# A recommender tower on one core: the first chunk's shifted rows and eight of its pair tiles made by TensorE instead of copied by DMA

## The chip, the cores and the metric

One core of one Trainium2 chip runs the program. The metric is the device time of one execution in microseconds, median over the runs. The core has TensorE (matmuls), VectorE, ScalarE and GpSimd, and SP, which only issues DMAs; ScalarE and GpSimd issue DMAs too. In the profile they are PE (PEld for its weight loads), DVE, ACT, POOL and SP.

## The reference

Each of 2048 rows of `ids` picks one row of 16 numbers from each of 39 tables. Three interaction layers follow, in which every pair of a field of the input and a row of the last layer's output is multiplied and summed with a weight:

```python
e = jnp.stack([tbl_0[ids[:, 0]], ..., tbl_38[ids[:, 38]]], axis=1)      # (2048, 39, 16)
x0 = xk = e
for idx, (W, b) in enumerate(params):                                   # W: (39, K, 128), K = 39, 64, 64
    z = jnp.einsum('bhd,bkd,hks->bsd', x0, xk, W) + b[None, :, None]
    z = jax.nn.relu(z)
    if idx != n_layers - 1:
        xk = z[:, :64, :]
        direct.append(z[:, 64:, :])
    else:
        direct.append(z)
logit = jnp.sum(jnp.concatenate(direct, axis=1), axis=-1)               # (2048, 256)
h = jnp.concatenate([logit, dense_ctx], axis=1)
h = jnp.maximum(h @ W_top1 + b_top1, 0.0)
h = jnp.maximum(h @ W_top2 + b_top2, 0.0)
y = h @ W_top3
```

All arrays are float32.

## The kernel before

The batch is cut into 16 groups of 128 rows, and each group into 4 chunks of 32 rows, so that a chunk has 32 times 16 = 512 columns. For a group, GpSimd gathers the 39 fields' rows into `emb` (128 partitions, one row of the batch each), one indirect DMA per field. SP stores `emb` into `x0_transposed` in HBM, in which a field is a row and batch times 16 are the columns. It has 39 rows and the first 20 of them once more, so that a block that is shifted by up to 20 fields can be read straight.

From there a chunk is loaded twice. `x0_diag` has 7 tiles for layer 0: three bands of 39 partitions, each holding the fields shifted by 0 to 20 (`diag_band`: SP loads two bands, ScalarE the third), and an eighth tile with the unshifted rows. `x0_pairs` has 20 tiles for layers 1 and 2: tile t holds field 2t in the upper 64 partitions and field 2t + 1 in the lower 64 (`pairs_half`: SP loads one half, ScalarE the other; SP also loads tile 19, which holds field 38 in all). There are two such buffers, for even and odd chunks.

VectorE multiplies four tiles at a time by `xk` (`product`), into a ring of four slots `prod`. TensorE multiplies them by weights and sums in `z`, in PSUM. Some tiles go as plain f32 (two passes each), others are split into a high part, rounded by ScalarE (`hi_parts`), and a low part, subtracted by VectorE or GpSimd (`lo_parts`), with three single passes. In layer 2 nearly all low parts are GpSimd's. The slots take their tiles in the order 0, 4, 16, 8, 12 (`FIRST_TILE`). TensorE's order in a chunk is layer 1 of this chunk, layer 0 of the next, layer 2 of this one. ScalarE turns a finished `z` into the next `xk` (`hand_on`), and every engine runs its own list in order and waits on semaphores.

GpSimd's gathers for the next group are set by numbers: `GATHERS_AHEAD` = 20 of group 1 come before its loop, and `GATHERS_AT` puts 10, 9, 10 and 10 into the four chunks of a group, each batch between its low part of layer 1 and its low parts of layer 2; the last two are for the group after.

Ahead of the loop the first chunk runs alone: SP stores group 0, waits for the store, loads the bands of chunk 0, waits for them and loads the pair tiles. VectorE and TensorE do layer 0 of chunk 0 in the meantime. The products of layer 1 wait for all pair tiles (`x0_pairs_in`) and for `xk1`.

## Time and profile before

| | us |
|---|---|
| median of 3 runs | 2450.69 (2449.82 to 2453.27) |
| profiled execution, its own time | 2460.42 |
| its span, first to last instruction | 2458.7 |
| TensorE busy | 2359.5 |
| VectorE busy | 2250.7 |
| GpSimd busy | 1710.2 |
| ScalarE busy | 1497.6 |

A span is the time from the first to the last instruction of the profiled execution, and the times of single instructions are counted from its start. Busy times leave out waits and the issuing of DMAs by SP and ScalarE. Matmuls overlap, so that the durations of single ones can add up to more than the time they take together; the chain counts each moment once.

### The profile page before, as it was taken

To read this page: it belongs to the slowest core of one execution; us is meant where nothing else is said; L and a number is where in the kernel's file an instruction comes from. 1 tells how busy PE (TensorE), PEld (TensorE's weight loads), DVE (VectorE), ACT (ScalarE), POOL (GpSimd) and SP (SyncE) were. 2 spreads that over 40 slices of the span, in tenths; PEclk is the share of its full clock that TensorE was granted. 3 is DMA by queue.
4 is the path that set the end of the run, shared out by engine and by line. 5 is a ranking of instruction groups with operands and counts; after the bars stand their busy time and mean duration, and the time that the engine had idled before them with its cause. 6 is when DMAs were issued, how large, how long until landed. Compare 5 with 4: busy or idle time off the path is not lost.

```text
span 2458.7 us, 26866 instructions
## 1 busy us (share of the span) xinstructions
PE 2359.5 (96%) x7768; PEld 1463.9 (60%) x7768; DVE 2250.7 (92%) x1383; ACT 1497.6 (61%) x1791; POOL 1710.2 (70%) x1091
## 2 busy tenths in 40 slices
PE   0499999999999999999999999999999999999999
PEld 0266666666666666666666666666666666666656
DVE  0499999999999999999999999999999999999983
ACT  0366666666666666666666666666666666666655
POOL 6577777777877777777777777677777767754540
PEclk9899999999999999999999999999999999999999
DMA  2887887878778787878878787887878788787730
GB/s 70 238 208 190 223 219 180 222 205 207 188 220 221 175 228 205 203 193 223 218 180 223 205 208 188 221 215 177 229 207 197 197 217 216 181 227 205 194 104 1
DMA packets 381242, 481.11 MB, mean 196 GB/s; under 512 B 140715, under 2 KB 155803, under 8 KB 381141
## 3 DMA queue, kind: packets, MB, share of 16 engines
q1 hardware_dynamic: 260294, 275.13, 44.4%
q10 hardware_dynamic: 100480, 200.29, 29.6%
q0 software_dynamic: 20448, 5.45, 1.9%
q8 instruction: 9, 0.15, 0.0%
q14 instruction: 11, 0.09, 0.0%
HBM read 470.96 MB, written 9.84 MB: 196 GB/s over the span
## 4 chain that ended last, share of the span: by engine, by line
PE 87%; POOL 4%; issue 4%; DMA 1%; DVE 1%; ACT 1%; SPq 0%; POOLq 0%; ACTq 0%; DVEq 0%
PE z L846 43%; PE z L825 42%; POOL lo_parts L273 4%; DVE prod L516 1%; PE z L963 1%; DMA x_pairs<-x_transposed 1%; PE xk L963 1%; ACT hi_parts L657 1%; POOL half_parts L267 0%; PE direct L963 0%; ACT xk L678 0%; DMA x_transposed<-emb 0%; ACT xk L677 0%; POOLq L139 0%; SPq L321 0%
## 5 line engine op out<-in xcount | busy, mean ns | idle before, releaser
L516 DVE TENSOR_TENSOR prod<-x_pairs,xk 128x2048 f32<-128x2048 f32 x640 | 1438.6, 2281 | 87.3 <-PE z L846 36.5
L825 PE MATMUL z<-prod,w_plain 128*128 128x512 f32 (+2 forms) x2688 | 1263.8, 594 | 93.5 <-DVE prod L516 93.4
L273 POOL TENSOR_TENSOR lo_parts<-prod,hi_parts 128x1024 fp32r<-128x1024 f32 x384 | 918.1, 2391 | 487.7 <-ACT hi_parts L657 462.4
L657 ACT CAST hi_parts<-prod 128x1024 fp32r<-128x1024 f32 x766 | 797.1, 1048 | 698.8 <-DVE prod L516 493.8
L846 PE MATMUL z<-hi_parts,w_lo 128*128 128x512 f32 (+1 forms) x1536 | 866.6, 564 | 3.2 <-POOL lo_parts L273 2.0
L446 POOL DMA_INDIRECT emb<-in_tbl,idx x624 | 702.5, 1126 | 195.5 <-issue 180.3
L825 PEld LDWEIGHTS z<-prod,w_plain 128*128 128x128 f32 (+2 forms) x2688 | 510.6, 190 | 492.5 <-issue 411.7
L846 PE MATMUL z<-hi_parts,w_hi 128*128 128x512 f32 (+1 forms) x1536 | 610.1, 397 | 0.0
L846 PE MATMUL z<-lo_parts,w_hi 128*128 128x512 f32 (+1 forms) x1536 | 606.8, 395 | 0.0
L846 PEld LDWEIGHTS z<-hi_parts,w_lo 128*128 128x128 f32 (+1 forms) x1536 | 289.9, 189 | 208.4 <-issue 146.1
L846 PEld LDWEIGHTS z<-lo_parts,w_hi 128*128 128x128 f32 (+1 forms) x1536 | 291.0, 189 | 191.4 <-issue 152.5
L846 PEld LDWEIGHTS z<-hi_parts,w_hi 128*128 128x128 f32 (+1 forms) x1536 | 288.8, 188 | 68.8
L273 DVE TENSOR_TENSOR lo_parts<-prod,hi_copy 128x1024 fp32r<-128x1024 f32 x256 | 310.2, 1212 | 12.7 <-ACT hi_copy L671 12.2
L516 DVE TENSOR_TENSOR prod<-x_diag,xk 117x2048 f32<-117x2048 f32 (+1 forms) x128 | 256.7, 2006 | 58.1 <-issue 58.1
L671 ACT CAST hi_copy<-prod 128x1024 fp32r<-128x1024 f32 x256 | 259.4, 1013 | 2.0 <-DVE lo_parts L273 0.3
L677 ACT ACTIVATE xk<-z,columns 64x512 f32<-64x512 f32 x128 | 83.0, 648 | 155.6 <-PE z L846 137.4
L273 DVE TENSOR_TENSOR lo_parts<-prod,hi_parts 117x1024 fp32r<-117x1024 f32 x128 | 150.1, 1210 | 0.0
L267 POOL TENSOR_TENSOR half_parts<-prod,half_parts 64x512 fp32r<-64x512 f32 x64 | 81.6, 1275 | 5.5
L678 ACT ACTIVATE xk<-z,columns 64x512 f32<-64x512 f32 x128 | 83.5, 652 | 1.6
L653 ACT CAST half_parts<-prod 128x512 fp32r<-128x512 f32 x128 | 78.5, 614 | 0.0
L701 ACT COPY xk<-x_diag 117x512 f32<-117x512 f32 x64 | 37.3, 583 | 59.4 <-DMA x_diag<-x_transposed 59.4
L846 PE MATMUL z<-half_parts,w_hi 128*128 128x512 f32 x128 | 50.8, 397 | 0.0
(75 smaller groups left out, 579.2 us busy)
## 6 DMA issues: line engine op xcount, KB each, us to landing
x_pairs<-x_transposed SPq DMA_DIRECT2D x64, 2432.0 KB
x_pairs<-x_transposed ACTq DMA_DIRECT2D x64, 2432.0 KB
x_diag<-x_transposed SPq DMA_DIRECT2D x128, 546.0 KB
x_diag<-x_transposed ACTq DMA_DIRECT2D x64, 546.0 KB
x_pairs<-x_transposed SPq DMA_DIRECT2D x64, 256.0 KB
emb<-in_tbl,idx POOLq DMA_INDIRECT x624
x_diag<-x_transposed SPq DMA_DIRECT2D x128, 78.0 KB
x_transposed<-emb SPq DMA_DIRECT2D x16, 312.0 KB, 6.1
```

What stands on the lines that cost most here:

```text
L267: engine.tensor_tensor(half_parts[0:HALF], held[0:HALF, at, :], hi, ALU.subtract).then_inc(done, 1)
L273: engine.tensor_tensor(lo_parts[0:rows, place:place + m, :], held[0:rows, at:at + m, :], hi, ALU.subtract).then_inc(done, 1)
L446: nc.gpsimd.indirect_dma_start(out=emb[:, f * D:(f + 1) * D], out_offset=None, in_=tables[f], in_offset=bass.IndirectOffsetOnAxis(ap=idx[: ...
L516: nc.vector.tensor_tensor(prod[0:rows, pos % RING, 0:n, :], a, xk.unsqueeze(1).broadcast_to([rows, n, N]), ALU.mult).then_inc(prod_ready, 1)
L653: nc.scalar.copy(half_parts[:], held[:, at, :]).then_inc(hi_ready, 1)
L657: nc.scalar.copy(hi_parts[0:rows, place:place + m, :], held[:, at:at + m, :]).then_inc(hi_ready, 1)
L671: nc.scalar.copy(hi_copy[:, 0:m, :].bitcast(F32R), held[:, at:at + m, :]).then_inc(hi_copied, 1)
L677: nc.scalar.activation(xk[0:HALF], z[layer][0:HALF], ACT.Relu, bias=b[0:HALF])
L678: nc.scalar.activation(xk[HALF:P], z[layer][0:HALF], ACT.Relu, bias=b[0:HALF]).then_inc(xk_ready[layer], 1)
L825: return nc.tensor.matmul(z[n][:], w, held[0:rows, i, :], start=first, stop=last)
L846: ins = nc.tensor.matmul(z[n][:], w, x, start=(first and i == 0), stop=(last and i == len(terms) - 1))
L963: ins = nc.tensor.matmul(acc[0:w.shape[1]], w, x, start=(k == 0 and not begun), stop=(k == len(terms) - 1))
```

## The change

In chunk 0 the seven shifted tiles of `x0_diag`, the unshifted rows for `xk0`, and tiles 12 to 19 of `x0_pairs` no longer come by DMA. TensorE transposes the first 32 rows of `emb` (16 small transposes into `z[1]`), VectorE copies the result to `rows0` (39x512), and TensorE multiplies `rows0` by matrices of zeros and ones, which pick for every output partition its field. Each result goes to one of three PSUM banks in turn, and ScalarE copies it to its tile. The matrices `by_diag` and `by_pair` are copied by VectorE out of `ident`, a twofold identity that GpSimd makes before its first gather. Tiles 0 to 11 are still copied by DMA, both halves from ScalarE's queue.

SP stores the first 32 rows of group 0 apart (`first_stored`), and the other 96 behind them; ScalarE's copies of tiles 0 to 11 wait for the first only. For later chunks nothing changes in how rows are stored and loaded.

Of group 1's gathers 14 instead of 20 come before the loop, 12 in chunk 0 and 13 in chunk 1. For that GpSimd's and VectorE's group 0 are written out ahead of their loops.

```diff
-GATHERS_AHEAD = 20
+GATHERS_AHEAD = 14
+GATHERS_FIRST = [range(14, 26), range(26, F), range(0, 10), range(10, 20)]
 GATHERS_AT = [range(20, 30), range(30, F), range(0, 10), range(10, 20)]
+SPREAD_PAIRS = (16, 17, 18, 19, 12, 13, 14, 15)
+COPIED_PAIRS = 12
+SPREAD_EARLY = 3
...
+        spread_banks = [z[1], hi_copy[:, 0, :], hi_copy[:, 1, :]]
+        spread_to = ([x0_diag[0:R0, t, :] for t in range(T0)]
+                     + [x0_pairs[0][:, t, :] for t in SPREAD_PAIRS])
...
+            def first_chunk():
+
+                sp.wait_ge(gathered, 16 * F)
+                store_rows(sp, 0, 0, slice(0, CB), first_stored)
+                store_rows(sp, 0, 0, slice(CB, P), xt_stored)
+                sp.wait_ge(xt_stored, 16 * ST_DMAS)
...
-            store_group(0)
-            sp.wait_ge(w0_summed, 2)
-            sp.wait_ge(w_split, 3)
-            load_chunk(0, 0)
+            first_chunk()
...
         def _(pool):
+            nc.gpsimd.memset(ident[:], 0.0).then_inc(ident_zero, 1)
+            for i in range(2):
+                pool.wait_ge(ident_zero, i + 1)
+                nc.gpsimd.affine_select(out=ident[:], in_=ident[:], compare_op=ALU.not_equal,
+                                        fill=1.0, base=i * F, pattern=[[-1, F + WRAP]],
+                                        channel_multiplier=1
+                                        ).then_inc((ident_zero, ident_ready)[i], 1)
...
             load_indices(1)
+            pool.wait_ge(first_stored, 16 * ST_DMAS)
+            pool.wait_ge(rows0_turned, 1)
             start_group(1, False)
             gather(range(0, GATHERS_AHEAD))
-            with pool.Fori(0, GROUPS - 2) as bt:
+            group(0, GATHERS_FIRST)
+            with pool.Fori(1, GROUPS - 2) as bt:
                 group(bt, GATHERS_AT)
...
+            dve.wait_ge(rows0_turned, 1)
+            nc.vector.tensor_copy(rows0[:], z[1][0:F]).then_inc(rows0_ready, 1)
             dve.wait_ge(xk0_ready, 1)
-            late, split = products(0, x0_diag, xk0, 0, 0, [], 0, 0)
+            late, split = products(0, x0_diag, xk0, 0, 0, [], 0, 0, {0: QUAD, 1: T0})
             subtract(late, split)
...
+            def take_spread(items):
+                for i in items:
+                    rows = spread_to[i].shape[0]
+                    act.wait_ge(spread, i + 1)
+                    nc.scalar.copy(spread_to[i], spread_banks[i % len(spread_banks)][0:rows]
+                                   ).then_inc(spread_ready, 1)
+
             act.wait_ge(weights_in, 16 * WEIGHT_DMAS)
-            act.wait_ge(xt_stored, 16 * ST_DMAS)
-            act.wait_ge(w0_summed, 2)
-            act.wait_ge(w_split, 3)
-            diag_band(nc.scalar, chunk_columns(0, 0), DIAG - 1)
-            copy_xk0(0)
-            pairs_half(nc.scalar, chunk_columns(0, 0), 0, 1)
+            act.wait_ge(gathered, 16 * F)
+            take_spread(range(0, 1))
+            act.wait_ge(first_stored, 16 * ST_DMAS)
+            for half in range(2):
+                src = xt[half:half + 2 * COPIED_PAIRS, 0:N].rearrange(
+                    "(t two) n -> t two n", two=2)[:, 0, :]
+                nc.scalar.dma_start(x0_pairs[0][half * HALF:(half + 1) * HALF, 0:COPIED_PAIRS, :],
+                                    src.partition_broadcast(HALF)).then_inc(first_pairs_in, 16)
+            take_spread(range(1, T0))
             for (k, at, m, _), place in zip(SPLITS[0], PLACES[0]):
...
+            take_spread(range(T0, T0 + SPREAD_EARLY))
             hand_on(0, xk1, b0_sb, SL0)
             direct_0()
+            take_spread(range(T0 + SPREAD_EARLY, len(spread_to)))
+            act.wait_ge(spread_ready, len(spread_to))
+            act.wait_ge(xt_stored, 16 * ST_DMAS)
             load_last_band(0, 1)
...
+            def spread_rows(items):
+                for i in items:
+                    if i >= len(spread_banks):
+                        pe.wait_ge(spread_ready, i + 1 - len(spread_banks))
+                    rows = spread_to[i].shape[0]
+                    nc.tensor.matmul(spread_banks[i % len(spread_banks)][0:rows], spread_by[i],
+                                     rows0[:], start=True, stop=True).then_inc(spread, 1)
+
+            pe.wait_ge(ident_ready, 1)
+            pe.wait_ge(gathered, 16 * F)
+            for d in range(D):
+
+                ins = nc.tensor.transpose(z[1][0:F, d:N:D], emb[0:CB, d:F * D:D], ident[0:CB, 0:CB])
+            ins.then_inc(rows0_turned, 1)
+            pe.wait_ge(chosen_ready, T0 + 3)
+            pe.wait_ge(rows0_ready, 1)
+            spread_rows(range(QUAD))
+            nc.tensor.matmul(xk0[0:R0], by_diag[:, T0, :], rows0[:], start=True, stop=True
+                             ).then_inc(xk0_ready, 1)
+            spread_rows(range(QUAD, T0 + SPREAD_EARLY))
             pe.wait_ge(w0_summed, 2)
             pe.wait_ge(w_split, 3)
             pe.wait_ge(weights_in, 16 * WEIGHT_DMAS)
             layer0(0, 0, {V: 0, G: 0})
+            spread_rows(range(T0 + SPREAD_EARLY, len(spread_to)))
+            pe.wait_ge(spread_ready, len(spread_to))
```

TensorE's list began with layer 0 of chunk 0 (the three rows of `w0_plain`). Now this stands ahead of it, from its first matmul on:

```order
L981 MATMUL z1<-ident,emb 39x32 x16
L974 MATMUL z1<-rows0,by_diag 117x512
L974 MATMUL hi_copy<-rows0,by_diag 117x512 x2
L974 MATMUL z1<-rows0,by_diag 117x512
L986 MATMUL xk2<-rows0,by_diag 117x512
L974 MATMUL hi_copy<-rows0,by_diag 117x512 x2
L974 MATMUL z1<-rows0,by_diag 117x512
L974 MATMUL hi_copy<-rows0,by_pair 128x512 x2
L974 MATMUL z1<-rows0,by_pair 128x512
L903 MATMUL z0<-prod,w0_plain 128x512 x3
```

Sixteen transposes and eleven matmuls of 512 columns now stand ahead of layer 0; five more stand behind it, ahead of layer 1.

ScalarE's list from the end of its weight casts to its first high part of the loop, before:

```order
L281 DMA x_diag<-x_transposed 39x7x512
L282 DMA x_diag<-x_transposed 39x512
L701 COPY xk<-x_diag 117x512
L287 DMA x_pairs<-x_transposed 64x19x512
L729 CAST hi_parts<-prod 117x1024 x2
L677 ACTIVATE xk<-z,columns 64x512
L678 ACTIVATE xk<-z,columns 64x512
L704 ACTIVATE direct<-z,columns 64x512
L281 DMA x_diag<-x_transposed 39x7x512
L282 DMA x_diag<-x_transposed 39x512
```

And now, from the first copy behind the casts of layer 0 on (lines 788 are copies of spread tiles, 741 and 742 the hand-on of `xk1`, 319 and 320 the band of chunk 1):

```order
L803 CAST hi_parts<-prod 117x1024 x2
L788 COPY x_pairs<-hi_copy 128x512 x2
L788 COPY x_pairs<-z 128x512
L741 ACTIVATE xk<-z,columns 64x512
L742 ACTIVATE xk<-z,columns 64x512
L768 ACTIVATE direct<-z,columns 64x512
L788 COPY x_pairs<-hi_copy 128x512 x2
L788 COPY x_pairs<-z 128x512
L788 COPY x_pairs<-hi_copy 128x512 x2
L319 DMA x_diag<-x_transposed 39x7x512
L320 DMA x_diag<-x_transposed 39x512
```

Five copies now stand between `direct_0` and the band of chunk 1, and three ahead of the hand-on.

GpSimd's list from its first gather to the low parts of layer 2 of chunk 0, before:

```order
L446 DMA emb<-in_tbl,idx 128x16 x39
L434 DMA idx<-in_ids 128x39
L446 DMA emb<-in_tbl,idx 128x16 x20
...
L273 TENSOR_TENSOR lo_parts<-prod,hi_parts 128x1024
L446 DMA emb<-in_tbl,idx 128x16 x10
```

And now, to those of chunk 1:

```order
L463 MEMSET ident 39x59
...
L466 AFFINE_SELECT ident<-ident 39x59 x2
L485 DMA emb<-in_tbl,idx 128x16 x39
L473 DMA idx<-in_ids 128x39
L485 DMA emb<-in_tbl,idx 128x16 x14
L290 TENSOR_TENSOR lo_parts<-prod,hi_parts 128x1024
L485 DMA emb<-in_tbl,idx 128x16 x12
L290 TENSOR_TENSOR lo_parts<-prod,hi_parts 128x1024 x3
L284 TENSOR_TENSOR half_parts<-prod,half_parts 64x512
L290 TENSOR_TENSOR lo_parts<-prod,hi_parts 128x1024 x3
L485 DMA emb<-in_tbl,idx 128x16 x13
```

Three instructions stand ahead of the first gather, and six of group 1's gathers moved from ahead of the first low part to behind it, two into chunk 0 and four into chunk 1.

## Rows read from the trace of the kernel before

**Rows 1.** The page, part 1: busy time, share of the span, instructions.

```profile
PE 2359.5 (96%) x7768; PEld 1463.9 (60%) x7768; DVE 2250.7 (92%) x1383; ACT 1497.6 (61%) x1791; POOL 1710.2 (70%) x1091
```

**Rows 2.** Timeline of GpSimd, 0 to 135 us: start, us, what [idle before].

```profile
3.00 1.08 POOL L446 DMA_INDIRECT emb<-in_tbl,idx  x1 [2.42 <-DMA idx<-in_ids]
...
52.34 0.94 POOL L446 DMA_INDIRECT emb<-in_tbl,idx  x1 [0.30 <-issue]
...
62.56 0.99 POOL L446 DMA_INDIRECT emb<-in_tbl,idx  x1 [7.04 <-DMA x_transposed<-emb]
...
108.61 2.36 POOL L273 TENSOR_TENSOR lo_parts<-prod,hi_parts 128x1024 fp32r<-128x1024 f32 x1 [20.35 <-ACT hi_parts L657]
...
111.13 0.96 POOL L446 DMA_INDIRECT emb<-in_tbl,idx  x1 [0.15 <-issue]
...
119.90 2.82 POOL L446 DMA_INDIRECT emb<-in_tbl,idx  x1 [0.31 <-issue]
...
126.08 7.36 POOL L273 TENSOR_TENSOR lo_parts<-prod,hi_parts 128x1024 fp32r<-128x1024 f32 x3 [0.85 <-ACT hi_parts L657]
```

**Rows 3.** Timeline of SP's queue, 0 to 135 us.

```profile
54.68 0.40 SPq L336 DMA_DIRECT2D x_transposed<-emb  x1
...
72.97 0.73 SPq L287 DMA_DIRECT2D x_pairs<-x_transposed  x1
```

**Rows 4.** Timeline of ScalarE and its DMA queue, 0 to 135 us.

```profile
72.98 0.59 ACT L701 COPY xk<-x_diag 117x512 f32<-117x512 f32 x1 [59.44 <-DMA x_diag<-x_transposed]
...
85.67 0.65 ACT L677 ACTIVATE xk<-z,columns 64x512 f32<-64x512 f32 x1 [7.76 <-PE z L846]
...
101.08 0.64 ACTq L287 DMA_DIRECT2D x_pairs<-x_transposed  x1
...
101.84 1.04 ACT L657 CAST hi_parts<-prod 128x1024 fp32r<-128x1024 f32 x1 [14.18 <-DVE prod L516]
```

**Rows 5.** Timeline of VectorE, 0 to 135 us.

```profile
73.60 3.95 DVE L516 TENSOR_TENSOR prod<-x_diag,xk 117x2048 f32<-117x2048 f32 x2 [58.06 <-issue]
...
98.59 4.49 DVE L516 TENSOR_TENSOR prod<-x_pairs,xk 128x2048 f32<-128x2048 f32 x2 [18.18 <-DMA x_pairs<-x_transposed]
```

**Rows 6.** Timeline of TensorE, its layer 0 parts in five places.

```profile
77.70 5.13 PE L825 MATMUL z<-prod,w_plain 117*128 117x512 f32 x6 [77.70 <-DVE prod L516]
...
120.89 2.74 PE L825 MATMUL z<-prod,w_plain 117*128 117x512 f32 x6
...
156.66 1.88 PE L825 MATMUL z<-prod,w_plain 117*128 117x512 f32 x4
...
1626.99 1.45 PE L825 MATMUL z<-prod,w_plain 117*128 117x512 f32 x3
...
1663.27 2.74 PE L825 MATMUL z<-prod,w_plain 117*128 117x512 f32 x6
```

**Rows 7.** The chain that ended last, 0 to 200 us: start, us, what.

```profile
121.06 2.58 PE z L825 x6
...
123.63 2.80 PE z L846 x12
```

**Rows 8.** Timeline of GpSimd, in chunk 1 and near 1633 us.

```profile
161.84 7.38 POOL L273 TENSOR_TENSOR lo_parts<-prod,hi_parts 128x1024 fp32r<-128x1024 f32 x3 [2.39 <-ACT hi_parts L657]
...
1632.84 7.37 POOL L273 TENSOR_TENSOR lo_parts<-prod,hi_parts 128x1024 fp32r<-128x1024 f32 x3 [1.65 <-ACT hi_parts L657]
```

**Rows 9.** Windows: length; busy us of PE, PEld, DVE, ACT, POOL; clock, DMA share, GB/s.

```profile
76.00:80.00 4.00, 2.30 (x3) 1.17 (x4) 3.89 (x4) 1.91 (x2) 3.08 (x4) 1.00 0.97 235
92.00:96.00 4.00, 0.00 (x0) 0.00 (x0) 0.00 (x0) 0.00 (x0) 0.00 (x0) 0.50 1.01 235
96.00:98.50 2.50, 0.00 (x0) 0.00 (x0) 0.00 (x0) 0.00 (x0) 0.00 (x0) 0.50 0.88 196
101.00:109.60 8.60, 8.09 (x12) 3.92 (x13) 7.72 (x5) 6.10 (x7) 0.99 (x1) 0.50 0.99 229
104.00:121.80 17.80, 17.29 (x50) 10.43 (x50) 17.80 (x12) 11.78 (x15) 10.90 (x9) 0.84 1.01 289
```

More of the change, by code:

```diff
@@ L274, in low_part, with chosen, store_rows @@
                                      hi, ALU.subtract).then_inc(done, 1)
+        spread_banks = [z[1], hi_copy[:, 0, :], hi_copy[:, 1, :]]
+        spread_to = ([x0_diag[0:R0, t, :] for t in range(T0)]
+                     + [x0_pairs[0][:, t, :] for t in SPREAD_PAIRS])
+        def chosen(first, *dims):
+            rows = ident[0:F, first:]
+            return bass.AP(tensor=rows.tensor, offset=rows.offset, ap=[rows.ap[0], *dims])
+        pair_columns = by_pair[:].rearrange("f g h -> f (g h)")
+        spread_by = ([by_diag[:, t, :] for t in range(T0)]
+                     + [pair_columns[:, (t - COPIED_PAIRS) * P:(t + 1 - COPIED_PAIRS) * P]
+                        for t in SPREAD_PAIRS])
+        def store_rows(engine, bt, first, parts, done):
+            cols = xt[:, bass.ds(first, P * D)].rearrange("f (b d) -> b f d", d=D)
+            rows = emb[:].rearrange("p (f d) -> p f d", d=D)
+            engine.dma_start(cols[parts, 0:F, :], rows[parts]).then_inc(done, 16)
+            engine.dma_start(cols[parts, F:F + WRAP, :], rows[parts, 0:WRAP, :]).then_inc(done, 16)
         def diag_band(engine, chunk, i):
@@ L349, in load_chunk @@
                     sp.wait_ge(xt_stored, 16 * ST_DMAS * (bt + 1))
-                if not (isinstance(bt, int) and bt == c == 0):
-                    sp.wait_ge(summed2, sums)
+                sp.wait_ge(summed2, sums)
                 chunk = xt[:, bass.ds(first, N)]
@@ L357, in load_chunk @@
                     store_group(bt + 1)
[L358 to L364 removed]
+                sp.wait_ge(prod_ready, slots)
                 pairs_half(sp, chunk, c, 0)
@@ L540, in splits_of, with products @@
                 return here
-            def products(n, copies, xk, slot, pos, late, split, chunk):
+            def products(n, copies, xk, slot, pos, late, split, chunk, spread_in={}):
                 first_tile, rows, tiles = (FIRST_TILE, P, TX) if n else (L0_FIRST, R0, T0)
                 for k, first in enumerate(first_tile):
+                    if k in spread_in:
+                        dve.wait_ge(spread_ready, spread_in[k])
                     product(slot + k, pos + k, copies[0:rows, first:min(first + QUAD, tiles), :],
@@ L582, in group @@
                     copies = x0_pairs[c % 2]
-                    dve.wait_ge(x0_pairs_in[c % 2],
-                                16 * X0_PAIRS_DMAS * (bt * (CHUNKS // 2) + c // 2 + 1))
+                    first = isinstance(bt, int) and bt == c == 0
+                    if first:
+                        dve.wait_ge(first_pairs_in, 32)
+                        dve.sem_inc(x0_pairs_in[0], 16 * X0_PAIRS_DMAS)
+                    else:
+                        dve.wait_ge(x0_pairs_in[c % 2],
+                                    16 * X0_PAIRS_DMAS * (bt * (CHUNKS // 2) + c // 2 + 1))
                     dve.wait_ge(xk_ready[0], chunk + 1)
-                    late, split = products(1, copies, xk1, slot, pos, [], split, chunk)
+                    spread_in = {FIRST_TILE.index(t): T0 + QUAD * (i + 1)
+                                 for i, t in enumerate(SPREAD_PAIRS[::QUAD])} if first else {}
+                    late, split = products(1, copies, xk1, slot, pos, [], split, chunk, spread_in)
                     slot, pos = slot + SLX, pos + SLX
@@ L604, in group @@
                     subtract(late, split)
-            with dve.Fori(0, GROUPS - 1) as bt:
+            group(0, False)
+            with dve.Fori(1, GROUPS - 1) as bt:
                 group(bt, False)
```

34 lines of the change are left out of this document (25 added, 9 removed).

## The prediction

> **What bounds the kernel now.** I read the page first. TensorE is busy 96% of the span [rows 1], so the middle of the run can only become shorter if TensorE gets less to do, and the change touches nothing there. The timelines of the first 135 us come next, with the wait ahead of each row in brackets at its end: TensorE waits 77.7 us for its first matmul [rows 6], and VectorE 18.2 us for the pair tiles of chunk 0 [rows 5]. Up to there it is a chain in which TensorE hardly works. GpSimd issues the 39 gathers one per 1.25 us from 3.00 to 53.3 [rows 2]; SP stores the rows at 54.68 and copies the pair tiles from 72.97, when the diagonal copies have landed [rows 3]; ScalarE copies `xk0` at 72.98 and hands `xk1` on with two activations from 85.67 to 87.0 [rows 4]; VectorE starts layer 0 at 73.60, but its first layer 1 product (call that moment T1) only at 98.59 [rows 5]. So `xk1` lay ready for 11.6 us: two things, the pair tiles and the layer 0 chain, must both come earlier.
>
> Behind T1 TensorE takes over. Its layer 0 part of the loop's chunks starts (call it s) at 120.89 and 156.66 [rows 6], 35.77 us apart. The chain gives the warm prices: 2.58 us for six f32 passes (0.43 each, two passes to a matmul) and 2.80 us for twelve of the others [rows 7]: 42 f32 passes and 76 others make 35.8 us, so no time is lost there. What the start saves is therefore kept to the end, unless GpSimd, whose low parts TensorE needs in layer 2, makes it wait. That margin is small and can be read. Let p be the start of GpSimd's first layer 2 low part. At s = 120.89, p is 126.08 [rows 2], p - s = 5.19, and the next s comes 35.77 later: no stall. At s = 1626.99, p is 1632.84 [rows 8], p - s = 5.85, and the next s is 36.28 later [rows 6]: 0.51 lost. So each us of p beyond s + 5.35 costs TensorE one us, and the next s is p + 30.4.
>
> **The change, part by part.**
>
> Removed: the diagonal copies of chunk 0 (54.7 to 73.0, behind the store), and 8 of 20 pair tiles. Left are 12 tiles by 128 partitions by 2 KB, 3.1 MB. While such copies ran alone the queues moved 235 GB/s [rows 9]: 13.4 us. They start when the first 32 rows are stored. Before, both stores had landed by 62.5 [rows 2], 7.9 us after the issue, for 128 rows; a quarter of the rows cannot take longer, nor less than the 0.9 us of two issues. I take 58.5 (about half of the 7.9), so the tiles are in at about 58.5 + 0.7 for the issue + 13.4 = 72.6, and at 76.6 if the store takes its full 7.9 us.
>
> Added ahead of T1, from 54.7 on:
> - Sixteen transposes. No row shows so small a matmul. Above, each is two passes of the 0.233 us kind (2.80 / 12), 7.5 us in all; below, they go by columns (32 of 512), 0.03 us each, 0.5 us in all. I take one such pass each, 0.2 us, nearer the upper row since each also loads its own weights: 3.2 us.
> - One VectorE copy of 39x512. The nearest row is ScalarE's copy of 117x512 at 0.59 us [rows 4]; with two handovers 0.9 us. So the spreads start at 58.8.
> - Ahead of layer 0, eleven f32 matmuls (seven shifted tiles, `xk0`, three pair tiles). Warm each is 0.86 us, 9.5 us. Cold they cost twice as much: the first six passes of the run before took 5.13 us [rows 6] against 2.58 warm [rows 7]. The granted clock stands at 1.00 there [rows 9], but a pass of 0.855 us is that of the 1.2 GHz level, and TensorE had done nothing until then. From there until TensorE's rate doubled it ran 4.5 us (77.70 to about 82.2); after the pause before T1 the column stands at 0.50, the 1.2 GHz level, and stays so to about 109.6 while TensorE works from 100.94 on [rows 9]. A slow spell of 4.5 us costs 2.25 us of work, one of 8.7 us costs 4.3. I take 2.5: 12.0 us, until 70.8. ScalarE's copies (0.6 us, three banks) are faster than the matmuls and hide beside them. VectorE's two layer 0 products (3.95 us together [rows 5]) wait for the fifth and eighth matmul and end at about 70.5, so they are hidden as well.
> - Layer 0 itself, warm: 2.58 + 2.80 = 5.4 us, until 76.2; the hand-on 1.4 us (85.6 to 87.0 before). T1 = 77.6. With the low ends (0.5 us, all warm) it is 72.4, when the tiles decide at 72.6; with the high ends (7.5 us, 4.3 us cold) 83.7.
>
> The Trainium skill (TensorE: Matmul & The Clock Gate, Part 4) says that transposes in transpose mode do not count as work for the clock gate. By that rule the matmuls behind them start cold, as in the trace's own first passes, and the sum stays as it stands; were the transposes to count, 3.2 us of the spell would pass under them, and T1 would be about 1.6 us earlier.
>
> Added behind T1. ScalarE still owes five copies when layer 0 ends. In order: hand-on to +1.3 us, `direct_0` to +2.0, three copies to +3.8, two more to +5.1 (TensorE makes them between +2.7 and +4.4). Its sequencer then waits for all 15 copies before it issues the diagonal pair of DMAs (about 0.9 us) and the pairs half (0.64 us [rows 4]), so the first high part begins at about +6.9, that is T1 + 5.5, where before it was 101.84 - 98.59 = 3.25 behind T1. VectorE's first low part waits for it: 2.25 us. From there VectorE works without a gap to 122 in the run before [rows 9], so the third product, and GpSimd's first low part with it, slips as much: from T1 + 10.0 [rows 2] to T1 + 12.3.
>
> Moved: six gathers of group 1 from ahead of the loop into chunks 0 and 1. GpSimd is ahead of time before T1, so there the six save nothing; in the chunks they lie right ahead of the low parts of layer 2. Chunk 0 had 10: from 111.13 to 125.23, 14.1 us (ten steps of 1.25 and one long gather of 2.82 us [rows 2]), and 0.85 us to spare. Twelve take 16.6. So p = T1 + 12.3 + 2.4 + 0.15 + 16.6 + 0.1 = T1 + 31.5, and the next s = T1 + 61.9. Before it was 156.66 - 98.59 = T1 + 58.1. Loss 3.8 us, the 2.25 above included. It also covers TensorE, which would otherwise start its first loop part 1 to 2 us late. Chunk 1 had 9 gathers and 2.39 us to spare [rows 8]; 13 take four more, 5.0 us, so p slips by 2.6 us, from s + 5.18 to s + 7.8, and 2.45 us are lost; with the L1 low part a little later, 2.6. From chunk 2 on the batches are those of before.
>
> The ten copies that VectorE gets ahead of the transposes and the three instructions of GpSimd ahead of the gathers I cost at nothing: VectorE idles for 58.1 us before 73.6 [rows 5], and GpSimd waits 2.42 us for the indices [rows 2]. Without that cover GpSimd's three would cost their own length, one for one. SP's and ScalarE's loads of chunk 1 are released by the same instructions as before and keep their distance to T1, so they stay hidden.
>
> **Sum.** T1: 77.6 - 98.6 = -21.0. Chunk 0: +3.8. Chunk 1: +2.6. Net -14.6 us. The profiled execution spans 2458.7 us and is timed at 2460.4, the median of the runs is 2450.7; the 10 us between lie over the whole run, so I subtract from the median: 2436.1. The changed profile's span should be about 2444.
>
> **The rivals.**
> 1. The copied pair tiles decide T1. For it: 64-byte stores of the other 96 rows and GpSimd's gathers run beside them, and the copies start no earlier than the first store lands. Against: 5 us of margin at my values. If the store takes its 7.9 us and the rate falls to the 196 GB/s of the last stretch before T1 [rows 9] (15.8 us), they land at 62.6 + 0.7 + 15.8 = 79.1: T1 +1.5; with 4 us of crowding by the store +5. Time 2438 to 2441. Chance 0.12.
> 2. TensorE's part is slow: transposes at their upper price and all eleven matmuls at 1.2 GHz, T1 = 54.7 + 7.5 + 0.9 + 18.8 + 5.4 + 1.4 = 88.7. Time up to 2447, likelier 2442. Chance 0.08.
> 3. GpSimd's new selects must first load code, and the gathers start late, one for one, beyond 2.42 us. Against: GpSimd's first elementwise instruction at 108.61 took 2.36 us, no more than a third of the three later ones' 7.37 [rows 2, 8], so nothing was loaded there. If a load came to twice the 2.42 us it would cost 2.4: 2438.5. Chance 0.06. The Trainium skill (GPSIMD Engine Reference, 2.1 Instruction dispatch) gives about 6 us for the first call to a freshly loaded kernel; by it the time would be about 2440.
> 4. Slower than before: ScalarE stands before `first_stored` with one tile copied, and TensorE has three banks; it stops after three matmuls until ScalarE goes on. Each us that the first store lands beyond about 62 then costs one. The whole gain is spent if it lands at 76, 22 us after its issue; 128 rows took at most 7.9. Time above 2451. Chance 0.02.
> 5. The mechanism holds but GpSimd, late twice, does not catch up with the index load of group 2, and further chunks lose as well. A loss like chunk 1's in each of the next four gives 10 us back: 2446. Against: the index load comes 22 us behind s and moves with it. Chance 0.04.
>
> **How the numbers follow.** The forecast, 2436.1, has 0.68, with T1 between 72.6 and 82: 2431 to 2441. The range for 8 in 10 adds most of rivals 1 and 3 above: 2430 to 2443. A difference under 0.2% (4.9 us) cannot be told from none. Faster by more takes the forecast and rivals 1 and 3, and most of 2: 0.93. Within it rival 5 and the rest of 2: 0.05. Slower: 0.02.
>
> **What the changed profile would show.** Transposes from 54.7, rows copy near 58, spreads to 71; the first layer 1 product at 77.6 and not released by a DMA; ScalarE's first high part 5.5 us behind it; p - s of about 7 and 8 in chunks 0 and 1, then 5.2; the waits of TensorE for GpSimd's low parts up by some 4 to 6 us in all. T1 beyond 84 would prove the chain wrong, p - s near 5.2 in chunk 1 the gathers' price.

## The result and the profile after

| | us |
|---|---|
| median of 4 runs, kernel before | 2450.94 (2449.82 to 2453.27) |
| median of 4 runs, changed kernel | 2440.08 (2439.63 to 2440.62) |
| ratio | 0.9958, interval 0.9946 to 0.9971 |
| profiled execution, its own time | 2440.03 |
| its span | 2438.3 |

The change saves 10.9 us of the predicted 14.6; the time lies inside the range of 2430 to 2443. The mechanism is the predicted one. One term of the sum, TensorE's slow spell, was far too small; the transposes were cheaper than taken, and some 5 us of the saving stand in no trace. So the number came into the range partly by luck.

The page's first part, against [rows 1]: TensorE is 13.5 us longer busy: 24.6 us more up to the first layer 0 part of the loop (52.0 against 27.4), and 11.1 us less behind it.

```profile
PE 2373.0 (97%) x7816; PEld 1466.3 (60%) x7816; DVE 2254.5 (92%) x1394; ACT 1505.0 (62%) x1805; POOL 1718.0 (70%) x1094
```

The timeline of TensorE to the first layer 1 product, against [rows 6] (start, us, what; the wait ahead in brackets). A row of x2 is one f32 matmul in two passes, a row of x4 two matmuls.

```profile
54.76 1.27 PE L981 MATMUL z<-ident,emb 32*39 32x32 f32 x16 [54.76 <-DMA emb<-in_tbl,idx]
56.89 2.02 PE L974 MATMUL z<-rows,by_diag 39*117 39x512 f32 x2 [0.87 <-DVE rows L626]
58.72 3.61 PE L974 MATMUL hi_copy<-rows,by_diag 39*117 39x512 f32 x4
...
70.66 3.61 PE L974 MATMUL hi_copy<-rows,by_pair 39*128 39x512 f32 x4
74.08 1.91 PE L974 MATMUL z<-rows,by_pair 39*128 39x512 f32 x2
75.92 5.13 PE L903 MATMUL z<-prod,w_plain 117*128 117x512 f32 x6
80.41 0.86 PE L924 MATMUL z<-hi_parts,w_lo 117*128 117x512 f32 x1
81.11 0.40 PE L924 MATMUL z<-lo_parts,w_hi 117*128 117x512 f32 x1
81.35 0.39 PE L924 MATMUL z<-hi_parts,w_hi 117*128 117x512 f32 x1
```

Read the starts, not the durations, since matmuls overlap. From 56.89 to 75.92 there are 22 passes in 19.0 us, 0.86 us each, the price of the 1.2 GHz level. The six passes of layer 0 cost the same (5.13, as in [rows 6]). Only from 80.4 on are the steps 0.23 us. TensorE had been at work for 23.5 us by then, without a pause after 56.9.

The same stretch in windows: length, busy us of each engine, and the granted clock behind POOL.

```profile
64.00:72.00 8.00, 8.00 (x11) 3.02 (x10) 2.77 (x2) 2.86 (x5) 2.32 (x3) 1.00 1.10 204
72.00:80.00 8.00, 8.00 (x10) 2.83 (x9) 4.03 (x4) 3.04 (x5) 6.17 (x7) 1.00 0.97 183
80.00:84.00 4.00, 4.00 (x15) 2.66 (x14) 0.00 (x0) 0.18 (x1) 3.07 (x4) 1.00 0.90 162
84.00:88.00 4.00, 4.00 (x9) 1.56 (x9) 2.84 (x2) 3.61 (x7) 1.89 (x2) 0.92 0.35 65
88.00:94.00 6.00, 5.03 (x6) 1.17 (x4) 1.65 (x1) 2.74 (x4) 0.00 (x0) 0.50 0.79 164
94.00:98.00 4.00, 2.62 (x10) 1.72 (x10) 3.75 (x3) 2.43 (x4) 0.00 (x0) 0.97 1.07 202
```

Between 64 and 80 the column says 1.00 and is not to be believed: some 19 passes in 16 us, with TensorE busy throughout, are the 1.2 GHz level (from 80 to 84 there are fifteen in 4 us). I take it that the column knows only changes; the first, by the passes, comes at 80.4, after 4.5 us of layer 0's 117 rows. From there on the column agrees with the passes. Note the fall between 84 and 94: layer 0 is over at 83.7, and TensorE goes on without a pause with the five late spreads, rows of 39.

VectorE, against [rows 5].

```profile
56.06 0.68 DVE L626 COPY rows<-z 39x512 f32<-39x512 f32 x1 [37.86 <-PE z L981]
65.78 2.29 DVE L558 TENSOR_TENSOR prod<-x_diag,xk 117x2048 f32<-117x2048 f32 x1 [9.04 <-PE xk L986]
71.52 1.75 DVE L558 TENSOR_TENSOR prod<-x_diag,xk 117x1536 f32<-117x1536 f32 x1 [3.45 <-ACT x_diag L788]
...
85.16 4.49 DVE L558 TENSOR_TENSOR prod<-x_pairs,xk 128x2048 f32<-128x2048 f32 x2 [9.03 <-ACT xk L742]
94.25 1.22 DVE L290 TENSOR_TENSOR lo_parts<-prod,hi_copy 128x1024 fp32r<-128x1024 f32 x1 [4.60 <-ACT hi_copy L735]
```

T1 is 85.16 instead of 98.59, and what it waits for is `xk1` of ScalarE, not a DMA. The first low part then waits 4.60 us for ScalarE, whose timeline follows, against [rows 4].

```profile
59.04 0.59 ACT L788 COPY x_diag<-z 117x512 f32<-117x512 f32 x1 [45.57 <-PE z L974]
59.06 1.43 ACTq L798 DMA_DIRECT2D x_pairs<-x_transposed  x2
...
83.82 0.65 ACT L741 ACTIVATE xk<-z,columns 64x512 f32<-64x512 f32 x1 [7.21 <-PE z L924]
...
89.43 0.59 ACT L788 COPY x_pairs<-hi_copy 128x512 f32<-128x512 f32 x1 [1.12 <-PE hi_copy L974]
90.04 0.60 ACTq L319 DMA_DIRECT2D x_diag<-x_transposed  x1
...
92.13 1.04 ACT L721 CAST hi_parts<-prod 128x1024 fp32r<-128x1024 f32 x1 [2.12 <-issue]
```

GpSimd, against [rows 2, 8]: selects, first gather of group 0, first gather of group 1, and the low parts of layer 2 in chunks 0 and 1.

```profile
1.26 0.60 POOL L466 TENSOR_SCALAR_AFFINE_SELECT ident<-ident 39x59 f32<-39x59 f32 x2 [0.24 <-POOL ident L463]
2.98 1.09 POOL L485 DMA_INDIRECT emb<-in_tbl,idx  x1 [1.12 <-DMA idx<-in_ids]
69.07 0.99 POOL L485 DMA_INDIRECT emb<-in_tbl,idx  x1 [13.59 <-DMA x_transposed<-emb]
...
117.23 7.51 POOL L290 TENSOR_TENSOR lo_parts<-prod,hi_parts 128x1024 fp32r<-128x1024 f32 x3
...
154.97 7.50 POOL L290 TENSOR_TENSOR lo_parts<-prod,hi_parts 128x1024 fp32r<-128x1024 f32 x3
```

And TensorE's layer 0 parts, from which s is read; the third follows at 185.69.

```profile
110.31 2.85 PE L903 MATMUL z<-prod,w_plain 117*128 117x512 f32 x6
147.98 2.74 PE L903 MATMUL z<-prod,w_plain 117*128 117x512 f32 x6
```

By these rows p is 6.92 and 6.99 behind s in the first two chunks, and the next s comes 37.67 and 37.71 later. Chunk 2 still takes 36.25; from the fifth chunk on most steps are 35.62.

### The profile page after: what moved, and what is told of

The parts are those of the page before. It is cut to its first block, busy times and chain, and to the rows that moved or that the text cites. A ratio compares the mean times of both kernels' runs of the same rounds, so it can differ in the third digit from the quotient of the medians.

```text
span 2438.3 us, 26914 instructions
## 1 busy us (share of the span) xinstructions
PE 2373.0 (97%) x7816; PEld 1466.3 (60%) x7816; DVE 2254.5 (92%) x1394; ACT 1505.0 (62%) x1805; POOL 1718.0 (70%) x1094
## 4 chain that ended last, share of the span: by engine, by line
PE 92%; POOL 4%; DVE 1%; issue 1%; DMA 1%; ACT 1%; POOLq 0%; ACTq 0%; DVEq 0%
PE z L903 45%; PE z L924 44%; POOL emb L485 2%; POOL lo_parts L290 2%; DVE prod L558 1%; PE z L1063 1%; PE xk L1063 1%; PE hi_copy L974 1%; DMA x_diag<-x_transposed 1%; PE direct L1063 0%; PE z L974 0%; ACT hi_parts L721 0%; DVE lo_parts L290 0%; POOL half_parts L284 0%; POOLq L143 0%
## 5 line engine op out<-in xcount | busy, mean ns | idle before, releaser
L290 POOL TENSOR_TENSOR lo_parts<-prod,hi_parts 128x1024 fp32r<-128x1024 f32 x384 | 927.6, 2416 | 456.2 <-ACT hi_parts L721 432.0
L924 PE MATMUL z<-lo_parts,w_hi 128*128 128x512 f32 (+1 forms) x1536 | 600.7, 391 | 0.0
L290 DVE TENSOR_TENSOR lo_parts<-prod,hi_copy 128x1024 fp32r<-128x1024 f32 x256 | 310.3, 1212 | 11.8 <-ACT hi_copy L735 5.9
L924 PE MATMUL z<-half_parts,w_lo 128*128 128x512 f32 x128 | 50.7, 396 | 0.0
```

What stands on the lines that cost most here:

```text
L290: engine.tensor_tensor(lo_parts[0:rows, place:place + m, :], held[0:rows, at:at + m, :], hi, ALU.subtract).then_inc(done, 1)
L924: ins = nc.tensor.matmul(z[n][:], w, x, start=(first and i == 0), stop=(last and i == len(terms) - 1))
```

## The experiments

The theory, called A below: TensorE's clock does not rise, and cannot be held, by matmuls whose operands have 39 rows, however close together they stand. The rival B: the clock would have risen, but started from idle, and matmuls ahead of the spreads would carry it over. Three groups of kernels ran, each group on one chip beside the kernel before. Where it matters the text says which.

### Spread operands of 128 rows

```diff
-        rows0 = sb("rows0", [F, N])
-        by_diag = sb("by_diag", [F, T0 + 1, R0])
+        rows0 = sb("rows0", [P, N])
+        by_diag = sb("by_diag", [P, T0 + 1, R0])
...
+            nc.vector.memset(rows0[:], 1.0).then_inc(wide_set, 1)
+            nc.vector.memset(by_diag[:].rearrange("p t r -> p (t r)"), 0.0).then_inc(wide_set, 1)
```

`by_pair` is treated alike. The 89 rows added are ones (in `rows0`) by zeros (in the matrices), so the sums stay the same. There are as many matmuls, with as many columns.

> The operands of the spread matmuls get all 128 rows instead of 39: below row 39 the moving operand holds ones and the matrices zeros, so the results are the same; VectorE's three fills lie in its idle time near 18 us. Theory A (the 39-row matmuls leave TensorE at 1.2 GHz, since it is the work in the array that raises its clock): the spreads start at 56.9, the passes take 0.85 us for 4.5 to 9 us and 0.43 after that, the eleven matmuls end at 68 to 71 instead of 75.9, layer 0 at 74 to 77, and the first layer 1 product starts at 78 to 79, held there by the pair tiles (their copies ran from 60.7 to 77.3). Time 6 us under the changed kernel, 2434. Rival B (the rows do not matter; two-pass matmuls in a row, or the pauses between them, keep the clock down): passes of 0.85 us up to layer 0 as before, first layer 1 product at 85.2, time 2440.

Measured: 2429.61 us, ratio 0.9917 (0.9903 to 0.9930) beside a kernel before at 2450.2. TensorE in this kernel:

```profile
53.61 1.27 PE L986 MATMUL z<-ident,emb 32*39 32x32 f32 x16 [53.61 <-DMA emb<-in_tbl,idx]
55.74 2.02 PE L979 MATMUL z<-rows,by_diag 128*117 128x512 f32 x2 [0.87 <-DVE rows L631]
57.57 3.11 PE L979 MATMUL hi_copy<-rows,by_diag 128*117 128x512 f32 x4
60.52 1.02 PE L979 MATMUL z<-rows,by_diag 128*117 128x512 f32 x2
...
67.53 2.81 PE L908 MATMUL z<-prod,w_plain 117*128 117x512 f32 x6
```

From 60.5 a matmul costs 0.86 us instead of 1.71, and layer 0 is at full rate from its first pass. The eleven spreads take 11.8 us (55.74 to 67.53), where I had 12.0, and 19.0 with 39 rows. The five late ones stay at full rate too (four passes in 1.98 us from 75.77, against 2.92 from 86.47 with 39 rows). A is confirmed for rows filled in this way. Whether it is their number or what they hold, no run tells: zeros in both operands were not tried. The time is 4.4 us under the 2434 expected; T1 came as expected, and 4.1 us were won between it and s (21.1 us instead of the changed kernel's 25.2). The next bound shows at once:

```profile
78.16 4.48 DVE L559 TENSOR_TENSOR prod<-x_pairs,xk 128x2048 f32<-128x2048 f32 x2 [7.86 <-DMA x_pairs<-x_transposed]
83.54 1.22 DVE L291 TENSOR_TENSOR lo_parts<-prod,hi_copy 128x1024 fp32r<-128x1024 f32 x1 [0.89 <-ACT hi_copy L740]
```

`xk1` was ready at 74.4; T1 waits for the copied pair tiles, my rival 1. ScalarE's late copies now fall into that wait, and its first high part is back at T1 + 3.26 (81.42).

> The kernel with spread operands of 128 rows once more, on one chip with the changed kernel. If the 39-row operands are what kept TensorE at its lower rate, it is 10 us (9 to 12) faster than after_again, at a ratio of 0.9917. If the gain of the first run came from something else of that chip, the two are equal.

> The changed kernel itself, as the base for the three others on the same chip. Expected 0.9958 of the kernel before, within 0.002; the first layer-1 product at 85 us, after the wait for xk1.

Measured, on one chip: 2430.55 us for it and, for the changed kernel run again, 2440.01. The ratios are 0.9921 (0.9908 to 0.9935) and 0.9962 (0.9948 to 0.9975), the kernel before 2449.74. So 9.5 us hang on the rows of the operands, though the matmuls are the same in number, columns and result. T1 was 78.83 and 84.96.

### Work ahead of the spreads

42 matmuls of 128x128x512 whose result nobody reads, started by GpSimd's 32nd gather:

```diff
+            pe.wait_ge(w_split, 3)
+            pe.wait_ge(nearly, 1)
+            for _ in range(42):
+                nc.tensor.matmul(z[1][:], w_hi[1][:, 0, :],
+                                 w_hi[1][:].rearrange("p t s -> p (t s)")[:, 0:N],
+                                 start=True, stop=True)
```

> TensorE multiplies 42 times 128x128 by 128x512 (results thrown away) in the last 11 us of the gathers; the spreads keep their 39 rows. Theory A: the clock is at its upper level when the transposes start at 54.8, and falls 3 to 4 us after the last full matmul although TensorE goes on with 39-row matmuls, as it fell 3.6 us after layer 0 in the changed kernel; so one to four passes are at 0.43 us and the rest at 0.85. First layer 1 product at 83 to 85, time 2438 to 2440. Rival B: the clock stays up as long as TensorE is busy at all, all spreads at 0.43 us, first layer 1 product at 78 (the pair tiles), time 2434.

> Both edits together. Theory A: all passes of the spreads at 0.43 us, eleven matmuls from 56.9 to 66.3, layer 0 ends at 72, xk1 is ready at 73.5, and VectorE now waits for the pair tiles until 78 to 79: the transfers and no longer TensorE set the first layer 1 product. Time like the wide kernel's or 1 us less, 2433. Rival C (the pair tiles are not what comes next, they were in much before 77): first layer 1 product at 73.6, time 2429.

Measured: 2438.73 (ratio 0.9952, 0.9939 to 0.9966) and 2429.62 (0.9918, 0.9904 to 0.9931). These tell nothing of B, by a fault in their design. The signal behind GpSimd's 32nd gather reached TensorE at 29.8, some 12 us before that gather's own row, so the matmuls came too early and left TensorE idle for 12.4 us:

```profile
29.82 12.68 PE L984 MATMUL z<-w_hi 128*128 128x512 f32 x42 [29.82 <-POOLq L524]
54.93 1.30 PE L990 MATMUL z<-ident,emb 32*39 32x32 f32 x16 [12.44 <-DMA emb<-in_tbl,idx]
```

With 98 of them there is no pause:

> As the warm kernel, which ended its full matmuls 12 us too early to tell anything, but with 98 of them, so that they last until about 54 us. Spreads at 39 rows. Theory A (39-row matmuls do not hold TensorE's clock up): it is at its upper level at the first spreads near 56.9 and falls 3 to 7 us after the last full matmul, near 58 to 61, so the first one to four passes take 0.43 us and the rest 0.85; first layer 1 product at 82 to 84.5, time 2437 to 2439. Rival B (any busy TensorE holds it): all passes 0.43 us, first layer 1 product at 78, time 2430 as the wide kernel.

Measured, on another chip, where the kernel before took 2466.34: 2470.41, ratio 1.0023 (1.0009 to 1.0036). The extra matmuls overran and held up the transposes by 6.5 us, so the time itself says little. The trace settles the question:

```profile
55.60 5.63 PE L984 MATMUL z<-w_hi 128*128 128x512 f32 x15 [0.84 <-issue]
61.16 1.28 PE L990 MATMUL z<-ident,emb 32*39 32x32 f32 x16
63.30 1.08 PE L977 MATMUL z<-rows,by_diag 39*117 39x512 f32 x2 [0.87 <-DVE rows L629]
64.22 1.88 PE L977 MATMUL hi_copy<-rows,by_diag 39*117 39x512 f32 x4
65.94 1.57 PE L977 MATMUL z<-rows,by_diag 39*117 39x512 f32 x2
67.31 1.91 PE L995 MATMUL xk<-rows,by_diag 39*117 39x512 f32 x2
...
79.39 4.79 PE L906 MATMUL z<-prod,w_plain 117*128 117x512 f32 x6
```

And its windows at 62 and 67, in the columns of above:

```profile
62.00:66.00 4.00, 3.13 (x14) 1.54 (x13) 0.68 (x1) 0.59 (x2) 1.92 (x2) 1.00 0.08 18
67.00:71.00 4.00, 4.00 (x6) 1.55 (x5) 1.75 (x1) 0.69 (x3) 3.00 (x4) 0.50 1.09 220
```

The spreads start at the 2.4 GHz level (0.43 a pass), and in the midst of them, with 39-row matmuls back to back, the granted clock falls to 0.50 and the passes go to 0.86. They stay there until layer 0. Ahead of the spreads stand the transposes and a pause of 0.87 us; the fall behind layer 0 in the changed kernel, above, has neither. So matmuls of 39 rows neither raise the clock nor hold it. B has fallen: warming saves 3 us, since the eleven spreads take 16.1 instead of 19.0 (63.30 to 79.39).

### Which pair tiles are copied

Two kernels: in `diag_only` all 20 tiles are copied and TensorE makes only the diagonal. `wide_copied16` is the wide kernel with 16 copied, and its edit is:

```diff
-SPREAD_PAIRS = (16, 17, 18, 19, 12, 13, 14, 15)
-COPIED_PAIRS = 12
+SPREAD_PAIRS = (16, 17, 18, 19)
+COPIED_PAIRS = 16
```

> One part of the change alone: TensorE makes the shifted rows, but all 20 pair tiles of chunk 0 are copied by DMA (three DMAs on ScalarE's queue behind the first store). Its queue moved 3.1 MB in 16.7 us in the changed kernel, 190 GB/s; 5.2 MB take 27.6 us from 60.7, so the first layer 1 product starts near 89 to 90 instead of 85.2, released by a DMA. ScalarE has no late copies, so its first high part lies 3.3 us behind that product, not 7.0, and 3.7 us of the 4 to 5 come back: time 2440 to 2441, the same as the changed kernel's. Rival: the eight tiles are what the change lives on, and without them the start is 8 us later: 2448.

> The wide kernel with tiles 0 to 15 copied and only 16 to 19 spread. If the copied tiles set its first layer 1 product (78.2, copies from 59.7 to 76.4), a third more bytes put it 5.5 us later, 83.7, and the time to 2434 to 2435, less up to 2 us because GpSimd's gathers of chunk 0 are then less late. Rival: the product waited for something else near 78 (the late copies of ScalarE); with four fewer of them it comes at 75 to 78: 2427 to 2430.

Measured, on the chip of 2466.34: 2463.70 (ratio 0.9993, 0.9984 to 1.0003) and 2459.10 (0.9974, 0.9964 to 0.9983). VectorE's first layer 1 product of the one and of the other:

```profile
89.18 4.48 DVE L558 TENSOR_TENSOR prod<-x_pairs,xk 128x2048 f32<-128x2048 f32 x2 [8.29 <-DMA x_pairs<-x_transposed]
```

```profile
87.42 4.49 DVE L559 TENSOR_TENSOR prod<-x_pairs,xk 128x2048 f32<-128x2048 f32 x2 [13.31 <-DMA x_pairs<-x_transposed]
```

Both wait for the copies, and T1 moves with their number: 12 tiles 78.2 (wide), 16 tiles 87.4, 20 tiles 89.2; behind the issue of the copies that is 20.3, 26.5 and 30.7 us. The issue of the 16 tiles came at 60.94, 3 us later than in wide, because VectorE copied the transposed rows only 3.2 us after the transposes; the profile puts that wait down to no engine of the core. T1 of `diag_only` is the one expected; that of `wide_copied16` was expected at 83.7. Both gained less in the time than expected (ratios of 0.996 and 0.9935).

With the diagonal alone T1 is 9.4 us before that of [rows 5] and the time the same as before. What the pair tiles are worth can't be read from the times, since the changed kernel was not run on this chip, and chunks there lose time in every kernel (below). The traces say more. Counted from SP's first store, the s of chunk 4 stands at 209.6 in the kernel before, 203.1 in the changed one and 204.4 in `diag_only` (264.24, 257.73 and 258.47 less 54.68, 54.64 and 54.06). So up to there the diagonal alone gives 5.2 of the 6.5 us, and the eight pair tiles, with 39 rows and late copies, 1.3. A surprise stood in `diag_only`, on ScalarE's queue:

```profile
58.49 1.80 ACTq L793 DMA_DIRECT2D x_pairs<-x_transposed  x2
60.33 9.14 ACTq L796 DMA_DIRECT2D x_pairs<-x_transposed  x1
69.51 1.07 ACT L784 COPY x_diag<-hi_copy 117x512 f32<-117x512 f32 x2 [10.46 <-issue]
```

The third DMA, tile 19, held ScalarE's sequencer for 9.14 us, so that the next copy came at 69.51 and the spreads, with three banks, stood still.

### When group 1 is gathered

The narrow kernel with the gathers of before, 20 ahead, then 10 and 9:

```diff
-GATHERS_AHEAD = 14
-GATHERS_FIRST = [range(14, 26), range(26, F), range(0, 10), range(10, 20)]
+GATHERS_AHEAD = 20
+GATHERS_FIRST = [range(20, 30), range(30, F), range(0, 10), range(10, 20)]
```

> Only the numbers of the gathers go back: 20 ahead of the loop, then 10, 9, 10, 10; the rest as changed. If the late low parts of GpSimd cost what the rule of the prediction says, p - s falls from 6.9 and 7.0 in chunks 0 and 1 to 5.2, and the 1.9 + 1.9 + 0.5 us that TensorE loses in chunks 0 to 2 come back: 2436. The 20 gathers run from 69.1 to 95.5 and end 3 us ahead of GpSimd's first low part at 98.9. Rival: they end late (another long gather) and hold that low part back, so that nothing is won: 2440.

Measured: 2435.45 (2434.94 to 2436.54), ratio 0.9941 (0.9928 to 0.9955), 4.6 us under the changed kernel's median; no run of the one reaches those of the other. They ran on two chips, on which the kernel before took much the same. By the traces 1.9 us of it is a T1 of 83.30, which the edit doesn't touch: the gathers ended 1.1 us earlier (transposes at 53.69), and TensorE's rate rose 0.8 us sooner in layer 0. Then 3.7 us fewer are lost in the first four chunks, and 1.4 us are given back between T1 and s, where TensorE is at 0.50 until past 97 and VectorE's first low part lies 0.8 us further behind T1. Splitting the gathers 14/12/13 therefore cost about what the prediction says of it (its chunk 1 and the two gathers of chunk 0 come to 4.2), and bought nothing: GpSimd still waited 3.72 us ahead of its first low part.

```profile
97.85 2.41 POOL L290 TENSOR_TENSOR lo_parts<-prod,hi_parts 128x1024 fp32r<-128x1024 f32 x1 [3.72 <-ACT hi_parts L721]
...
115.57 7.51 POOL L290 TENSOR_TENSOR lo_parts<-prod,hi_parts 128x1024 fp32r<-128x1024 f32 x3 [1.90 <-ACT hi_parts L721]
```

The same on wide operands, where T1 is earlier and the cover smaller, with 16/11/12 and 20/10/9:

> Wide spread operands, and of group 1's gathers 16 instead of 14 ahead of the loop, 11 and 12 in chunks 0 and 1. In wide GpSimd idles 2.53 us ahead of its first low part (88.19), room for two gathers of 1.25. By the rule that each us of the first layer-2 low part beyond s + 5.35 costs TensorE one, chunk 0's distance of 8.05 falls by 1.25 and chunk 1's 6.77 by 1.25: 2.5 us faster than wide_again, about 2427. The rival, that these gathers do not matter to the time, says equal to wide_again.

> Wide spread operands with the gathers of the kernel before: 20 ahead of the loop, 10 and 9 in the first two chunks. Now the batch ahead of the loop is too long: 68.5 + 20 x 1.25 = 93.5 instead of 88.19 for the first low part, 5.3 us late, against 2.5 saved by two gathers fewer in chunk 0 and 1.9 in chunk 1. The rule gives a first layer-2 low part near 110 instead of 107.3; time about that of wide_again or 1 us more, 2430 to 2431, and 3 us more than wide_gathers16. The rival, the fewer gathers inside the chunks the better (as it was with the narrow operands, where 20 gave 4.6 us), gives 2425.

Measured, on the chip of 2449.74: 2430.05 (2428.44 to 2436.07) and 2432.82 (2427.55 to 2433.02), ratios 0.9928 (0.9914 to 0.9941) and 0.9926 (0.9912 to 0.9939), beside wide's 0.9921 (by the medians 0.9920, 0.9931 and 0.9922). No version beats wide; the 2.5 us expected of the first did not show in the time. Its scatter of 7.6 us would hide them. The traces are clearer. The rule on p holds in each (p from GpSimd's timeline, the next s from TensorE's):

| kernel, chunk | p - s | p | next s | difference |
|---|---|---|---|---|
| changed, 0 | 6.92 | 117.23 | 147.98 | 30.75 |
| changed, 1 | 6.99 | 154.97 | 185.69 | 30.72 |
| 20/10/9, 0 | 5.76 | 115.57 | 146.30 | 30.73 |
| wide, 0 | 8.05 | 107.30 | 137.99 | 30.69 |
| wide, 1 | 6.77 | 144.76 | 175.45 | 30.69 |
| wide 16/11/12, 0 | 5.71 | 107.29 | 138.01 | 30.72 |
| wide 20/10/9, 0 | 6.87 | 109.50 | 140.24 | 30.74 |

Relative to T1, the s of chunk 4 comes 1.9 us earlier with 16/11/12 than in wide_again and 0.9 us earlier with 20/10/9. So the gathers did what was expected of them behind T1. With 16/11/12 it was given back by a T1 0.6 us later (79.40 against 78.83) and small losses in the rest of the run (2.4 us between chunk 4 and the end). Whether these are the kernel's or the execution's is open.

The last kernel of this kind gathers group 1 into columns of `logit` that are free in group 0, so that GpSimd need not wait for the stores of `emb`:

```diff
+            pool.wait_ge(idx_in, 16)
+            pool.sem_inc(waits_held, 1)
+            gather(range(0, GATHERS_AHEAD), True)
...
-                        out=emb[:, f * D:(f + 1) * D], out_offset=None, in_=tables[f],
+                        out=held_apart(f, 1) if apart else emb[:, f * D:(f + 1) * D],
+                        out_offset=None, in_=tables[f],
```

SP stores group 1 from there, in three pieces, and its group 0 is written out ahead of its loop.

> The wide kernel, with group 1 gathered into unused columns of logit01 and logit2 instead of emb, so that GpSimd need not wait until group 0 is stored (it waited to 69 in the changed kernel), and with the gathers back at 20, 10, 9, 10, 10. The 20 gathers run from 60 to 86, ahead of the first low part at 88.5. If the wide kernel's losses in chunks 0 to 2 (3.1 + 1.9 + 0.7 us by its TensorE starts) come from the late gathers alone, they shrink to under 1: time 2424 to 2425. Rival: the copies of the pair tiles share the queues with more gathers and the first product slips by as much: 2429.

Measured, on the chip of 2466.34: 2465.83, ratio 0.9999 (0.9990 to 1.0008), a miss. The gathers did start at 58.13, but ScalarE handed `xk1` on only at 85.01, though TensorE had finished layer 0 near 74:

```profile
85.01 0.65 ACT L770 ACTIVATE xk<-z,columns 64x512 f32<-64x512 f32 x1 [14.80 <-remote]
```

What held ScalarE for those 11 us isn't settled; the profile names no engine of the core, as for the 3 us of `wide_copied16` on the same chip. The second loss is the edit's own. GpSimd gathers group 2 only when group 1 has been stored out of `logit`, and the stores wait for one another: it waited 8.22 us for them, until 182.63, where wide gathers from 166.64. So in chunk 2 p - s rose to 12.73 and 8.9 us were lost. (SP's loads of the pairs, behind these stores, took 10.38 and 4.71 us to issue.) Both eat the gain, so this run doesn't tell whether gathers that need not wait would help.

## Why the prediction was right, and where its sum was off

**What bounds the kernel now**: right for the start. T1 fell by 13.4 us and the time by 10.9. "So no time is lost there" for the middle was too bold, see below. The prediction's own sign of a wrong chain, T1 beyond 84, did appear (85.16): the order of the chain held, but one of its terms did not. Of the other signs, T1 was indeed not released by a DMA, p - s was 6.92 and 6.99 where it said about 7 and 8, and TensorE's waits for GpSimd's low parts rose by 1.8 us (2.0 to 3.8) and not by 4 to 6.

**The slow spell, the step that was mis-sized.** The prediction says "I take 2.5: 12.0 us, until 70.8", with 4.3 as the upper end. The eleven spreads took 19.0 us, and layer 0 from 75.92 to 83.7 another 7.8 instead of 5.4. Together that is 26.8 instead of 17.4: 9.4 us, more than the 7.6 by which T1 missed 77.6. The price of a pass was right; what failed was taking the length of the spell from a stretch in which TensorE worked on 117 and 128 rows. The wide kernel, whose spreads do have such operands, took the 12.0 predicted (11.8). Rival 2, all eleven at 1.2 GHz with T1 at 88.7, was the case in truth as far as the clock goes; it had 0.08. Its other half, dear transposes, did not come. The Trainium skill (TensorE: Matmul & The Clock Gate, Part 1) says that activity of TensorE releases the throttle. The trace agrees only for operands of 117 or 128 rows (the rate doubled at 80.4, in layer 0); 39 rows back to back for 19 us released nothing. Whether transposes count, the question that the prediction took from the page, was of no weight beside it.

**Transposes and the rows copy.** 1.27 us for sixteen (3.2 taken, bounds 0.5 and 7.5), and 0.9 for the copy with its handovers (56.03 to 56.89), as taken. Two us better, and with them T1's miss is accounted for: 9.4 - 1.9 = 7.5.

**The copied pair tiles** came later than 72.6: in wide they release T1 at 78.16, 20 us after their issue at 57.91. The first store did land as taken (58.5; the DMAs are issued at 59.06, behind ScalarE's copy), but all traffic together moved 183 to 204 GB/s between 64 and 80, not 235. The 96-row store of SP runs beside them: its last part, issued at 56.28, landed 11.9 us later, and GpSimd's gathers, which wait for it, go on at 69.07 (before at 62.56). When the tiles landed in the changed kernel no row says, since nothing waited for them. With the 20 us of wide they were in at about 79, which is past the 77.6 of the forecast: the 5 us of margin were gone, and only the slow spell kept rival 1 from deciding T1. It does in wide.

**Behind T1.** ScalarE's first high part came at T1 + 6.97, not + 5.5: the last two of the five late spreads, from 86.47, took 2.92 us for four passes, since the clock fell again, and the three DMA issues behind the last copy took 2.0 us instead of 1.5. Chunk 0's next s is T1 + 62.8 (61.9 predicted), 4.7 us lost instead of 3.8. Chunk 1 lost 1.9 (37.71 less 35.77) instead of 2.6, with p - s = 6.99 instead of 7.8; chunk 2, costed at nothing, 0.5. Sum: 7.1 instead of 6.4. The rule itself was 0.3 short (next s = p + 30.7 instead of 30.4).

**What does not add up.** -13.4 and +7.1 give -6.3, and the medians say -10.9. The two profiled spans differ by 20.4 (2458.7 and 2438.3; the prediction had 2444 for the second). The traces of the changed kernel and of wide close among themselves: the changed kernel is 7.0 us later at T1, 4.1 more at the first s of the loop, 0.8 less over the next four chunks and 1.1 more over the rest, in all 11.4, and the spans differ by 11.4. So the gap lies with the kernel before. Its profiled execution stood 9.7 us over its median: it stepped by 35.77 where nine profiled executions, those of the changed kernel among them, step by 35.6, and lost 5.8 us more in scattered chunks between the fifth and the 57th, where those nine lost 0.6 to 2.1 and the four on the chip of 2466.34, counted against steps of 35.6, 19 to 26. Taking both out of its profile would put it at about 2446, not 2450.7. Some 5 us of its median are therefore in no trace that I have, and the prediction's landing in the range was luck in so far: with its own terms right it would have said -6, that is 2444.6, outside its range. Where the 5 us were stays open. The kernel before has one trace only, so its step of 35.77 may be that execution's or the kernel's own; if it is in part the kernel's, the change also saves time in the middle, where the prediction says that it touches nothing.

**GpSimd's selects** cost 0.60 us for two, inside the wait for the indices (1.12 left), and no code was loaded: rival 3 is out. Rival 4 did not come near, and of rival 5 only chunk 2's 0.5 us came. Rival 1 is answered above.

## What to carry to other kernels

Before small matmuls take over a TensorE start-up, ask what clock they run at: if their operands have few rows (39 here), take the slow price for all of them and for the first passes of what follows, or fill the rows up. Here that was ones against weights of zero; it cost three memsets in VectorE's idle time and gave 9.5 us. When one load is taken off the path, work out the landing time of the next with the traffic that now runs beside it, here 64-byte stores. And make the balance against a profiled execution whose time is that of the median; a profile 10 us above it hides terms of the size that are to be predicted.
